# Paged attention scores as four 32-row products, and the new rows' values laid out by DMA

## The reference, cut to what matters

```python
q = _rope(_rms(q, q_norm_scale), pos)          # 8 heads of 32
k = _rope(_rms(k, k_norm_scale), pos)          # 4 groups of 32
k_blocks = k_blocks.at[blk, :, off, :].set(k)  # new rows go into the pages
v_blocks = v_blocks.at[blk, :, off, :].set(v)
scores = jnp.einsum('bghtd,bgsd->bghts', qg, k_all) * SCALE   # SCALE = 1/16
allowed = (kpos <= pos) & (kpos > pos - WINDOW)
p = jax.nn.softmax(jnp.where(allowed, scores, -inf), axis=-1)
o = jnp.einsum('bghts,bgsd->bghtd', p, v_all)
return o @ Wo.T
```

## Time and profile before

| | |
|---|---|
| runs shown | 591.44, 592.98, 593.17 us |
| median | 592.98 us |
| profiled execution | 592.35 us, its span 590.6 us |
| PE, DVE, ACT, POOL busy | 492.1, 368.2, 243.1, 260.7 us |
| granted TensorE clock, mean | 0.908 of full |

### The profile page before, as it was taken

How to read it: one execution, slowest core, us unless ns; L and a number is a source line. 1 busy time by engine, 2 the same in 40 slices (tenths; PEclk the granted TensorE clock), 3 DMA queues, 4 the chain that set the end, 5 groups by cost and what they waited for, 6 DMA issues and landing times. The chain is left out here.

```text
span 590.6 us, 10701 instructions
## 1 busy us (share of the span) xinstructions
PE 492.1 (83%) x4141; PEld 363.5 (62%) x4141; DVE 368.2 (62%) x780; ACT 243.1 (41%) x525; POOL 260.7 (44%) x240
## 2 busy tenths in 40 slices
PE   2968799999999899989869889559989893089966
PEld 0445547888688688866554436437766592079956
DVE  3736747888587788865776554967778447034422
ACT  6025865443333334341674443356655241024430
POOL 5014833465343588764570000178880105526650
PEclk9979599999999999999969999859999877579987
DMA  4991026000000022221000006711000001297516
GB/s 169 380 409 63 1 81 199 0 1 1 1 0 1 18 63 63 57 76 67 2 2 2 1 1 255 271 44 27 23 24 3 2 0 54 95 356 233 175 61 208
DMA packets 24433, 51.49 MB, mean 87 GB/s; under 512 B 4232, under 2 KB 16673, under 8 KB 23488
## 3 DMA queue, kind: packets, MB, share of 16 engines
q1 hardware_dynamic: 18416, 40.60, 19.3%
q0 software_dynamic: 5968, 10.22, 5.6%
HBM read 43.97 MB, written 12.37 MB: 95 GB/s over the span
## 5 line engine op out<-in xcount | busy, mean ns | idle before, releaser
L706 PE MATMUL ps<-x_split,gate_up_split 128*128 128x512 f32 x384 | 96.3, 393 | 0.1
L706 PEld LDWEIGHTS ps<-x_split,gate_up_split 128*128 128x128 f32 x384 | 72.0, 188 | 17.1 <-issue 1.5
L1970 POOL DMA_INDIRECT wbig<-new_kv,prepi x40 | 42.1, 1052 | 76.5 <-DMA new_kv<-work 65.4
L899 POOL TENSOR_TENSOR gate_up_split<-wbig,gate_up_split 128x768 fp32r<-128x768 f32 (+1 forms) x24 | 41.5, 1731 | 52.0 <-ACT gate_up_split L839 51.9
L821 DVE TENSOR_TENSOR hidden_split<-work,hidden_split 128x512 fp32r<-128x512 f32 x34 | 37.8, 1113 | 23.1 <-ACT hidden_split L888 23.1
L888 ACT ACTIVATE hidden_split<-work 128x512 fp32r<-128x512 f32 x34 | 21.4, 629 | 60.3 <-DVE work L816 60.3
L730 PE MATMUL ps<-hidden_split,down_split 128*128 128x512 f32 x160 | 42.5, 395 | 3.0 <-issue 1.4
L1911 POOL DMA_INDIRECT chosen<-work,wbig x31 | 30.5, 984 | 29.1 <-issue 15.0
L905 POOL TENSOR_TENSOR down_split<-wbig,down_split 128x384 fp32r<-128x384 f32 (+1 forms) x24 | 29.1, 1212 | 26.2 <-ACT down_split L846 26.1
L608 POOL TENSOR_TENSOR work<-work,prep 128x512 f32<-128x512 f32 x16 | 16.7, 1046 | 52.8 <-DVE prep L488 52.2
L1970 POOL DMA_INDIRECT wbig<-in_cache_dram,prepi x32 | 33.5, 1047 | 7.7 <-issue 7.4
(11 more groups left out here) (327 smaller groups left out, 1157.8 us busy)
## 6 DMA issues: line engine op xcount, KB each, us to landing
work<-in_wE_dram SPq DMA_DIRECT2D x1, 5376.0 KB, 17.3
wbig<-in_wF_dram SPq DMA_DIRECT2D x1, 4992.0 KB, 20.3
sorted<-wmid SPq DMA_DIRECT2D x1, 3999.0 KB, 14.7
wbig<-in_wG_dram SPq DMA_DIRECT2D x1, 3072.0 KB, 27.2
wbig<-in_wE_dram SPq DMA_DIRECT2D x6, 384.0 KB, 4.3
wbig<-chosen SPq DMA_DIRECT2D x8, 256.0 KB, 4.7
wbig<-sorted SPq DMA_DIRECT2D x1, 1935.0 KB, 14.4
wmid<-in_wE_dram SPq DMA_DIRECT2D x5, 384.0 KB, 8.4
```

Of the source, the lines that this page charges most:

```text
L706: mm = nc.tensor.matmul(o, self.gus[:, w % 2, a, 2 * m + k, :], self.xs[:, b, k, n * HALF:(n + 1) * HALF], start=(k == 0 and a == b), stop ...
L899: nc.gpsimd.tensor_tensor(self.gus[:, k % 2, 1, 0:self.gu_chunks], self.gate_up[:, :, j * P:(j + 1) * P], self.gus[:, k % 2, 0, 0:self.gu_ ...
L1970: return nc.gpsimd.indirect_dma_start(dst, None, table, bass.IndirectOffsetOnAxis(ap=rows.bitcast(U32), axis=0), **({} if bound is None el ...
```

## The change

Scores: each of the four groups gets a product of its own, over the 32 partitions that hold its features, on queries that aren't masked. The four products of a sequence use four different row quarters of the array; groups 0 and 2 write the upper half of the output partitions, groups 1 and 3 the lower half; groups 0 and 1 go to one bank, 2 and 3 to the next. The mask goes into the two banks with two products of 128 rows and 160 columns in place of one of 32 rows and 320 columns; `token_r` becomes four tiles that are zero outside one quarter, made by four operations on GpSimd in place of one. The 16 masking operations go; ScalarE makes four plain scaled copies (`keep_queries`).

Order: PE's transposes of query half 1 come after `scores(0)`; ScalarE's `root("q", 1)` and `keep_queries(1)` come after `keep_keys(0)`. The scores take four banks (2 to 5), so `turn` has bank 6 alone and waits for the copy of the sequence before it (`page_pT` at b, formerly b - 1), and `turn_last` uses bank 1.

New rows' values: GpSimd clears `vlast` once (128x1024) and SP's queue copies the four quarters of each tile onto its diagonal, 4 DMAs of 32x128 for each group of four, 32 in all.

```diff
-        qmask = cut(work, 0, 8192).rearrange("p (b g h t) -> p b g h t", b=B, g=GRP, h=2)
+        qT_page = cut(work, 6144, 2048).rearrange("p (b h t) -> p b h t", b=B, h=2)
...
             def scores(b):
...
-                j = slice(32 * (b % 4), 32 * (b % 4) + 32)
-                nc.tensor.matmul(ps[:, 2 + b % 2, 0:2 * NKEY].rearrange("p (a j) -> p a j", a=2), token_r[j, :],
-                                 masks[j, b // 4, :].unsqueeze(1).to_broadcast([32, 2, NKEY]), start=True, stop=False)
+                bank = 2 + 2 * (b % 2)
                 for a in range(2):
-                    mm = nc.tensor.matmul(ps[:, 2 + b % 2, a * NKEY:(a + 1) * NKEY],
-                                          qmask[:, b, 2 * a:2 * a + 2, :, :].rearrange("p g h t -> p (g h t)"),
-                                          kTs[b // 4 % 2][:, b % 4, :], start=False, stop=(a == 1))
+                    nc.tensor.matmul(ps[:, bank + a, 0:NKEY], token_r[:, b % 4, :], masks[:, b // 4, :], start=True, stop=False)
+                for g in range(GRP):
+                    r, q = slice(32 * g, 32 * g + 32), slice(64 * (g % 2), 64 * (g % 2) + 64)
+                    mm = nc.tensor.matmul(ps[q, bank + g // 2, 0:NKEY], qT_page[r, b].rearrange("p h t -> p (h t)"),
+                                          kTs[b // 4 % 2][r, b % 4, :], start=False, stop=True)
...
             def turn(b):
                 pe.wait_ge(sem("page_norm"), 2 * (b + 1))
-                if b >= 2:
-                    pe.wait_ge(sem("page_pT"), b - 1)
+                if b:
+                    pe.wait_ge(sem("page_pT"), b)
+                else:
+                    pe.wait_ge(sem("page_qm"), 4)
...
             def values(q4):
...
-                pe.wait_ge(sem("page_vlast"), q4 + 1)
+                pe.wait_ge(sem(f"page_vlast{q4 % 2}"), 64 * (q4 // 2 + 1))
...
+            queries(0)
             keys(0)
+            pe.wait_ge(sem("page_qm"), 2)
+            pe.wait_ge(sem("page_table"), 10 + B // 4)
+            pe.wait_ge(sem("page_token"), 4)
             scores(0)
+            queries(1)
...
-            for n in range(2):
-                dve.wait_ge(sem("page_qt"), 2 * n + 1)
-                for g in range(GRP):
-                    nc.vector.tensor_scalar(qmask[:, 16 * n:16 * n + 16, g, 0, :],
...
+            root("q", 0)
+            keep_queries(0)
             keep_keys(0)
+            root("q", 1)
+            keep_queries(1)
...
+            sp.wait_ge(sem("vlast_zero"), 1)
+            for q4 in range(B // 4):
+                sp.wait_ge(sem(f"overlay{q4 % 4}"), 16 * 5 * (q4 // 4 + 1))
+                if q4 >= 2:
+                    sp.wait_ge(sem("page_pv"), q4 - 1)
+                for b in range(4):
+                    rows = slice(32 * b, 32 * b + 32)
+                    sp.dma_start(vlast[rows, q4 % 2, b, :], kv[rows, B + q4, P:2 * P]).then_inc(sem(f"page_vlast{q4 % 2}"), 16)
...
+            pool.wait_ge(sem("att_proj_done"), 2 * ATT_TOTAL["proj_done"])
+            nc.gpsimd.memset(vlast.rearrange("p r b f -> p (r b f)"), 0.0).then_inc(sem("vlast_zero"), 1)
...
-                if n % 5 == 4 and n >= 10:
-                    last_values(n // 5 - 2)
-            last_values(B // 4 - 2)
-            last_values(B // 4 - 1)
```

More of the change, by code:

```diff
@@ L1331, in program @@
         plastT = cut(wmid, 1280, 512).rearrange("p (r a q) -> p r a q", r=2, a=2)
-        vlast = cut(wmid, 1792, 1024).rearrange("p (r b f) -> p r b f", r=2, b=4)
+        vlast = cut(wmid, 2048, 1024).rearrange("p (r b f) -> p r b f", r=2, b=4)
         pex = cut(wmid, 5120, 960).rearrange("p (r a j) -> p r a j", r=3, a=2)
@@ L1412, in page_tensor, with queries @@
                         mm.then_inc(sem("page_proj"), 1)
-            for n in range(2):
+            def queries(n):
                 pe.wait_ge(sem("page_rot"), n + 3)
@@ L1428, in keys @@
                     pe.wait_ge(sem("page_kT"), 2 * q4)
+                if q4 >= 2:
+                    pe.wait_ge(sem("page_lT"), q4 - 1)
                 for j in range(4):
@@ L1508, in page_vector @@
                     rotate(dve, name, n)
-            for n in range(2):
-                dve.wait_ge(sem("page_qt"), 2 * n + 1)
-                for g in range(GRP):
-                    nc.vector.tensor_scalar(qmask[:, 16 * n:16 * n + 16, g, 0, :],
-                                            ps[:, n, :].rearrange("p (b t) -> p b t", t=S),
-                                            const("quad16")[:, g:g + 1], None, ALU.mult).then_inc(sem("page_qm"), 1)
             def before(b):
                 dve.wait_ge(sem("page_scores"), b + 1)
-                nc.vector.tensor_reduce(pst[:, b, 0:2], ps[:, 2 + b % 2, 0:2 * NKEY].rearrange("p (a j) -> p a j", a=2),
-                                        AXX, ALU.max, negate=True).then_inc(sem("page_max"), 1)
+                bank = 2 + 2 * (b % 2)
+                nc.vector.tensor_reduce(pst[:, b, 0:2], ps[:, bank:bank + 2, 0:NKEY], AXX, ALU.max, negate=True).then_inc(sem("page_max"), 1)
             def after(b):
@@ L1577, in page_scalar, with keep_queries @@
                 copies("q", n, Q_AT, 0)
-            for n in range(2):
-                root("q", n)
-            act.wait_ge(sem("page_rot"), 4)
-            for n in range(2):
-                act.wait_ge(sem("page_qt"), 2 * n + 2)
-                for g in range(GRP):
-                    nc.scalar.activation(qmask[:, 16 * n:16 * n + 16, g, 1, :],
-                                         ps[:, 2 + n, :].rearrange("p (b t) -> p b t", t=S), ACT.Copy,
-                                         scale=const("quad16")[:, g:g + 1]).then_inc(sem("page_qm"), 1)
+            def keep_queries(n):
+                for hh in range(2):
+                    act.wait_ge(sem("page_qt"), 2 * n + hh + 1)
+                    nc.scalar.activation(qT_page[:, 16 * n:16 * n + 16, hh, :],
+                                         ps[:, 4 + 2 * n + hh, :].rearrange("p (b t) -> p b t", t=S), ACT.Copy,
+                                         scale=1.0 / 16).then_inc(sem("page_qm"), 1)
             def keep_last(q4):
@@ L2059, in _ @@
             nc.gpsimd.memset(pdiag.rearrange("p r h q -> p (r h q)"), 0.0).then_inc(sem("zeroed"), 1)
-            nc.gpsimd.tensor_copy(token_r, const("token")).then_inc(sem("page_token"), 1)
+            for j in range(4):
+                nc.gpsimd.tensor_scalar(token_r[:, j, :], const("token"), const("quad")[:, j:j + 1], None, ALU.mult)\
+                    .then_inc(sem("page_token"), 1)
             pool.wait_ge(sem("cached"), 16 * B)
             att_b.gpsimd(pool)
+            pool.wait_ge(sem("att_proj_done"), 2 * ATT_TOTAL["proj_done"])
+            nc.gpsimd.memset(vlast.rearrange("p r b f -> p (r b f)"), 0.0).then_inc(sem("vlast_zero"), 1)
             pool.wait_ge(sem("prep_step"), N_PREP)
@@ L2066, in _ @@
             pool.wait_ge(sem("page_new"), 32)
-            def last_values(q4):
-                pool.wait_ge(sem(f"overlay{q4 % 4}"), 16 * 5 * (q4 // 4 + 1))
-                if q4 >= 2:
-                    pool.wait_ge(sem("page_pv"), q4 - 1)
-                nc.gpsimd.tensor_tensor(vlast[:, q4 % 2], kv[:, B + q4, P:2 * P].unsqueeze(1).to_broadcast([P, 4, P]),
-                                        const("quad").unsqueeze(2).to_broadcast([P, 4, P]), ALU.mult)\
-                    .then_inc(sem("page_vlast"), 1)
             pool.wait_ge(sem("page_rot"), 2)
```

20 lines of the change are left out of this document (9 added, 11 removed).

## The result

The changed kernel takes 1.0064 of the time before (95% interval 1.0037 to 1.0092); that is 3.8 us more (2.2 to 5.5). The ratio leaves out runs more than 1.5% above the fastest of the same kernel, by this rule eight of 20 before and one of 20 after; over all 20 runs each the means differ by only 1.8 us and the medians (600.25 and 599.29) by 1.0, so the size is less sure than its interval. The forecast was +0.3%; the sign was right, the size less than half of the ratio's. One kernel's runs spread over 591 to 605 us with their mean granted clock (of the changed kernel, 593.48 us at 0.908 and 603.64 at 0.889). The profiled execution took 599.88 us, span 598.0.

A forecast was written before the change was run, and what follows sets the result against it. It took VectorE's pace between groups and PE's key and value block as bounds; 0.6 + 1.9 - 1.1 + 0.35 = +1.75 on 592.35 gave 594.1, or 594.7 since that execution lay 0.63 below the median; range 590.5 to 607.

The forecast's parts named there:

- Start, +0.6: Start of the stage: maskings gone, square root moved behind key copies; first exponential 1.8 later, mark b = 3 0.6 later.
- Clock back at 406 instead of 401, +1.9: PE's clock after the start: pauses delay its return to about 406 from 401.2, at 0.4 per us, +1.9 us.
- b = 3 near 404.8: Sign to look for: the reduction of sequence 3, at 402.30 before, stands near 404.8.
- clock low in the loop: Rival, chance 0.17: PE's clock stays at 1.2 GHz in loop groups, 11 us each instead of 7.55; 602 to 619 us.
- Loop, -1.1: Sequences b = 3 to 31: six groups of 7.55 (5.17 through transposes, 2.37 block) plus 7.0 make 52.3 against 53.45.
- wait hidden: Faster rival, chance 0.16: `turn`'s wait also hidden before keys and values; groups 7.0, loop 48.5, time 590.9 us.
- Tail, +0.35: Behind the last reduction mark: the last `turn` has the same wait for the copy, +0.35 us.
- Mask price 0: PE's two mask products per sequence: lower bound 0.11 each taken; dear-mask rival, chance 0.16, put +3 us, 597.7.
- one bank side by side: Four score products run together despite shared banks; rival, chance 0.05, had two of four queue, +2.5 us, 597.2.
- GpSimd's multiplication, 2.9: In the old loop it lengthened VectorE's small multiplication: three groups by 0.5 and one by 1.5, 2.9 us in all.
- SP's transfers, 0: The 32 DMAs on SP's queue are issued a group (7 us) before use, so they cost 0.
- Clearing `vlast`, 0: GpSimd's clearing after the attention before, when it is idle; cost 0, at worst holding VectorE 0.9.

The follow-up runs named there:

- e4: Changed kernel with PE's and ScalarE's work at the start back in the old order; ratio 0.9999 to the kernel before.
- e12: The changed kernel itself timed once more, in a batch where signals were late; ratio 1.0477 to the kernel before.
- e1: Changed kernel with the new rows' values made by GpSimd's multiplication again (new scores alone); ratio 1.0014 to the kernel before.
- e3: Changed kernel with the last `turn` of each group writing bank 7, so it needn't wait for the copy before; ratio 0.9881 to the kernel before.
- e13: Changed kernel with bank 7 for each group's last `turn`, old start order and GpSimd's old values; ratio 0.9995 to the kernel before.
- e14: Changed kernel with bank 7 for each group's last `turn`, old start order and GpSimd's multiplications into an unread spare tile; ratio 0.994 to the kernel before.
- e11: Kernel before with only the values by SP's transfers, old scores, in a batch where signals were late; ratio 1.0349 to the kernel before.
- e2: Kernel before with only the new rows' values changed (GpSimd clears once, SP copies the quarters); ratio 0.9947 to the kernel before.
- e15: Changed kernel with bank 7 for each group's last `turn`, old start order and no SP transfers (new rows' values left out); ratio 0.9817.
- e16: Changed kernel with bank 7 for each group's last `turn` and the old start order; ratio 0.9816 to the kernel before.
- e18: Changed kernel with bank 7 for each group's last `turn`, old start order, no SP transfers, timed where signals were late; ratio 1.021.
- e17: Changed kernel with bank 7 for each group's last `turn`, old start order, GpSimd's multiplications into a spare tile, timed where signals were late; ratio 1.012.
- e6: Changed kernel with bank 7 for each group's last `turn`, old start order and 31 identity transposes in PE's early waits; ratio 1.0388.

## Why the prediction was wrong in size

*Start, +0.6: right.* The first exponential moved by 1.52 (forecast 1.8), b = 3 by 0.57. The square root ran 13.5 behind the mark of the table above, 13.8 forecast (392.3). By e4 this +0.57 is a gain of 3.0 less a loss of 3.6 through the moved order.

*Clock back at 406 instead of 401, +1.9: wrong.* It came back at 408.53, 23.89 behind the mark; before it was 22.72. So it returned 1.2 later and not 4.8. The groups behind b = 3 are 7.68 and 7.69 from the first on: all of this low clock lies ahead of b = 3, where the 0.57 already holds it, and the forecast's own sign (b = 3 near 404.8, +2.5) failed with it. The price for each us was near: 3.4 us of low clock in the loop made a group 1.29 longer, 0.38 for each us against the 0.4 of the estimate, and in e12, where the clock is low for the first 5.1 us of the loop, the first group is 8.98, 0.25 for each. So "clock low in the loop" happened once, for 3.4 us. In e1, e3 and e4, with the same products, and in e12's groups behind the clock's return (452.7: 7.68 to 7.88, the last 7.14) it doesn't come back. e13 has two such stretches and e14 three, so what brings one stays open.

*Loop, -1.1: the step that failed.* The forecast had the wait of `turn` in the right place and gave it too small a price. With the dear group put at 7.69 the loop is 6 x 7.69 + 7.14 = 53.28, -0.2; as profiled, with the low clock in that group, it is +1.17. The forecast's 5.17 + 2.37 = 7.55 became, in the group from 424.37 to 432.12, 5.26 to the end of the transposes (429.63) and 2.49 for the block. The wait for `turn_last` was put at 0.2 and measured 0.41, and the block lost not 0.36 but about 0.24. The size of the whole wait is what was mis-read: between the 7.0 of "wait hidden" and 7.55 it was 0.55, by e3 it is 0.78 a group. The rival's 7.0 was good, e3 measures 6.91: it failed only because the wait is bare. The products themselves came out near: 0.29 less for each sequence (0.86 against 1.15), 0.36 forecast.

*Tail, +0.35: right.* At full clock `wo` starts 5.36 after b = 31 in e12 and 4.97 in e11 with the old scores, +0.39; the 0.69 of the profiles has low clock in it.

*Mask price 0, one bank side by side: right.* Mask records are 0.159 apart (0.11 was the lower bound taken, 0.2 the sign of being wrong), the four products start within 0.03 us, two to a bank; this is what the forecast took from the earlier trace rows against the Trainium skill, TensorEngine Tiling (Array Packing), "Gotcha 1: PSUM Pressure". By the page two of the four would have queued, +2.5; the trace does not show it. The two products of a bank write different halves of the partitions here; products of one bank that write the same partitions are not tested.

*GpSimd's multiplication, 2.9: right in the old loop* (e2: 2.92), and the saving is in the 53.28.

*SP's transfers, 0: right* (e15 against e16).

*Clearing `vlast`, 0: open.* Behind it the clock falls in every trace, and 2.70 of the changed kernel's profile is lost there. For its being a cost speaks e1, which doesn't clear, with a stage sum near the changed kernel's (+2.1 and +2.43) and a ratio of 1.0014. Against it speaks e2, which clears and whose timing (-3.2) leaves no room beside its stage sum (-3.0).

The sum with measured sizes is 0.57 - 0.17 + 0.39 = +0.8 at full clock, +2.43 with the profile's own low stretches; the timing says +3.8 (2.2 to 5.5). That the forecast's +1.75 has the right sign is in part luck: its two errors, 1.9 too much for the clock and 0.9 too little for the loop, work against each other. The 1.4 between +2.43 and +3.8 is shown in no stage. It may be the fall of the clock behind the clearing, or no time at all, since the means over all runs differ by 1.8. What the forecast had no term for is the lateness with which signals arrive while the gathers run.

## What to carry to other kernels

When a buffer is made single, look for what stands behind the new wait in the engine's queue: here it was bare at one place in four, and cost more than the faster products gave back. One bank in the right place gave 0.78 of 7.69 us a group. With the old start order too the change becomes a gain (0.9816), but only where signals aren't late: the same kernel was 1.0341 and 1.0278 in the two batches where they were. Two engines that slow each other cost little while a wait for a third sets the pace (0.2 for a multiplication of 1823 ns in e1), and much (4.7 us in e13) as soon as it doesn't: price such a contention in the new loop, not in the old. And read the trace ahead of the stage that was changed: a clearing put at 0 stood in front of a fall of the clock that none of the sums has.

## What was not expected of the hardware

In three of five batches VectorE and ScalarE stood ready for up to 28 us for products of TensorE that were over (e18: 3.8, 8.8 and 27.6), while GpSimd issued its gathers, one each 1.30 us. The kernel before was 12 to 20 us slower in these batches (611.9 to 616.9 against 597.3 to 600.3), presumably by it, though it has no trace there; the changed one was 40 us slower (640.0 in batch 3 against 600.3). GpSimd's multiplication between the gathers, a cost of 4.7 us in batch 4 (e13), went with a gain of 8.2 in batch 5 (e17 against e18 at `wo`). 31 transposes of 128x128 in PE's waits held the granted clock at 2.4 GHz 6.7 us past the mark and not longer (e6: 1.2 GHz from 390.1 to 451.5); PE was idle for 3.92 when it fell.
